# Squares two granules later, loads of weight pairs five granules behind their stores, and the threshold search's last sixteen bits every third granule

## The chip, the cores and the metric

The kernel runs on one core of one Trainium2 chip. The metric is the device time of one execution in microseconds (us), given as the median of three runs. One further execution was recorded by the hardware profiler, and all rows below come from it.

## What is computed

2048 tokens of 1024 values are normalised (xn) and go through two feed-forward networks, whose results are added to the token.

```python
s = silu(xn @ w_gate.T)                      # 2752 values a token
s = where(|s| among the 1376 smallest, 0, s) # per token
a = (s * (xn @ w_up.T)) @ w_down.T

shared = (relu(xn @ up_w) ** 2) @ down_w     # 2048 values a token
routed = ((xn @ fc1_w) @ expert_w * (sum of the two largest of xn @ gate_w)) @ fc2_w
y = x + a + layernorm(shared + routed) * gamma + beta
```

## The kernel before

**Blocks and granules.** The tokens are taken in four blocks of 512 (four tiles of 128). In each block TensorE goes through the same list `STEPS` of 212 granules. A granule is one slab of 128 rows by 512 columns of a weight and takes twelve matmuls (three for each tile: every 32-bit operand is held as a high part and a low part, and the products high by high, high by low and low by high are added). The steps that matter here, with their first granules: gate 0 to 5 from 0, latent 48, hidden 0 and 1 from 56, routed 72, shared 0 and 1 from 80, hidden 2 and 3 from 96, up 4 at 112, shared 2 and 3 from 120, up 0 at 136, up 1 at 144, up 2 at 152, up 3 at 160, out 0 at 168, out 1 at 190. Successive steps use PSUM banks 0 to 3 and 4 to 7 in turn, so up 2 can begin on its banks only when VectorE has read those of up 0.

**The weight pairs.** In block 0 a granule's weight arrives raw (a ring of `RAW` = 4) and is split into its two parts in a slot of the ring `w` (`RING` = 6 slots). ScalarE makes the high part (line 474), but for granules 52 to 167 GpSimd makes it (line 443); GpSimd always makes the low part (line 447) and signals `lo_ready`. SyncE's queue issues every transfer (lines 383 to 414): for each granule of block 0 it waits for `lo_ready`, loads the raw slab four granules ahead and stores the pair in DRAM (line 347, into `split_w`). Blocks 1 to 3 load the pairs from there (line 353) into the slot of the granule six before, once TensorE has read it; for the first six granules of block 1 that load also waits for the slot's own store.

**The other engines** run a loop over the same granule numbers m, each in its own order, and wait on semaphores; a number m on them is a place in their order, not a time. Results of a step that ends at granule e are read at m = e + 4 (`LAG`). `granule_read` is the wait for TensorE's reading.

- Squares of hidden values (`HIDDEN_AT`, m = 68, 70, ... 82 and 108, 110, ... 122, sixteen a block): ScalarE squares into the high part at m (line 531), GpSimd squares the same at full precision at m (line 452) and VectorE subtracts at m + 1 for the low part (line 935). TensorE's shared granules wait for that low part one by one (`hidden_lo`).
- The search (`SEARCH_AT`): 31 bits of a threshold for each token, one bit a step, starting at m = 52. In each step VectorE makes a candidate (line 808) and counts for tiles 0 and 1 (line 813, two passes), ScalarE counts for tiles 2 and 3 at m and m + 1 (line 486), and VectorE settles the bit (lines 798 and 801) at the next step's place. Bits 0 to 14 are three granules apart, the later ones three and four in turn, so that bit 30 is at 150 and `SEARCH_END` is 153.
- At `SEARCH_END` VectorE looks for ties (`drop_ties`, four counting passes at line 821 and a few small operations), then come the masks (`MASK_AT`, line 875), with up's results read in between (`READ_UP_AT`, line 788: up 4 at 123, up 0 at 147, up 1 at 155, up 2 at 163, up 3 at 169). Masks 4, 5, 0, 1 and 2 are at 154, 155, 156, 157 and 164.
- From m = 163 on GpSimd multiplies the masked values (line 463), TensorE turns them (line 606), ScalarE and VectorE take them back (lines 579 and 973), four granules ahead of out 0, which uses them.

Of the kernel before, what the change touches and what calls it, by code (L numbers as in the profile page):

```python
# [33 lines left out]
TILES = N // P  # L34
BLOCKS = TOKENS // N
# [9 lines left out]
RING = 6  # L45
RAW = 4
LAG = 4
BITS = 31
# [100 lines left out]
SEARCH_AT = {END[("gate", GC - 1)] + LAG + 1: 0}  # L149
while len(SEARCH_AT) < BITS:  # L150
    _last = max(SEARCH_AT)
    SEARCH_AT[_last + 3 + (len(SEARCH_AT) % 2 if len(SEARCH_AT) >= BITS // 2 else 0)] = len(SEARCH_AT)
SEARCH_FROM, SEARCH_END = min(SEARCH_AT), max(SEARCH_AT) + 3
MASK_AT = {max(SEARCH_END + 1 + i, END[("up", g)] + LAG + 1 if g < GC - 1 else 0): g
           for i, g in enumerate(GROUPS[:-1])}
# [4 lines left out]
assert len(GATED_AT) == GK and len(MASK_AT) == GC  # L160
READ_HIDDEN_AT = {END[("hidden", i)] + LAG: ("hidden", i) for i in range(SC)}
HIDDEN_AT = {END[("hidden", i)] + LAG + 1 + 2 * t: (i, t) for i in range(SC) for t in range(TILES)}
GPSIMD_HI = list(range(SEARCH_FROM, OUT0))
NORM_AT = [OUT0 + 6 + 3 * t for t in range(TILES)]
TOKENS_AT = [OUT0 + 20, OUT0 + 21, OUT1 + 10, OUT1 + 14]
# [9 lines left out]
def granule_read(eng, granule_used, bank_filled, b, m):  # L175

    if m in ENDS:
        name = next(s for s in END if END[s] == m)
        eng.wait_ge(bank_filled, filled(b, (*name, TILES - 1)))
    else:  # L180
        eng.wait_ge(granule_used, released(b, m))
# [19 lines left out]
def program(nc, x, w_gate, w_up, w_down, up_w, down_w, fc1_w, expert_w, fc2_w, gamma, beta, routed_w, y):  # L201
    ctx = ExitStack()
    with ctx:
# [133 lines left out]
        @block.sync  # L337
        def _(sp):
            def load_raw(m):
                src, width = source(m)  # L340
                if m == START[("routed", 0)]:
                    sp.wait_ge(routed_stored, 32)
                sp.dma_start(raw[:, m % RAW, 0:width], src).then_inc(raw_loaded[m % RAW], 16)

            def store_split(m):
                width = source(m)[1]
                sp.dma_start(split_w[m, :, :, 0:width],
                             w[:, m % RING, :, 0:width].bitcast(F32)).then_inc(split_stored[m % RING], 16)

            def load_split(g):  # L350
                m, r = g % GRANULES, g % RING
                width = source(m)[1]
                sp.dma_start(w[:, r, :, 0:width].bitcast(F32), split_w[m, :, :, 0:width]).then_inc(split_loaded[r], 16)

            def load_rows(b, t):
                sp.dma_start(rows_of(t), x[(b * TILES + t) * P:(b * TILES + t + 1) * P, :])\
                  .then_inc(rows_loaded[t % 2], 16)

            def store(b, i, t):

                s = slice(i * N, (i + 1) * N)
                bank, value = emptied(b, ("out", i, t))
                sp.wait_ge(bank_emptied[bank], value)
                sp.dma_start(y[(b * TILES + t) * P:(b * TILES + t + 1) * P, s], acc[:, t, s]).then_inc(stored, 16)

            for t in range(2):
                load_rows(0, t)
            for k in range(LK):
                sp.dma_start(expert_raw[:, k, :], expert_w[k * P:(k + 1) * P, :]).then_inc(first_loaded[k], 16)
                sp.dma_start(fc2_raw[:, k, :], fc2_w[k * P:(k + 1) * P, :]).then_inc(first_loaded[k], 16)  # L370
            for t in range(2, TILES):
                sp.wait_ge(bank_filled, FIRST_AT[("token", t - 2)] + 2)
                load_rows(0, t)
            for m in range(RAW):
                load_raw(m)
            sp.dma_start(gamma_all[:, :], gamma.to_broadcast([P, HID])).then_inc(consts_loaded, 16)
            sp.dma_start(beta_all[:, :], beta.to_broadcast([P, HID])).then_inc(consts_loaded, 16)
            for h in range(2):
                s = slice(h * N, (h + 1) * N)
                for t in range(LK):  # L380
                    sp.wait_ge(bank_emptied[4 + t], 2 + h)
                sp.dma_start(routed_w[:, s].rearrange("(k p) n -> p k n", p=P), acc[:, :, s]).then_inc(routed_stored, 16)
            for b in range(BLOCKS):
                for m in range(GRANULES):
                    if b == 0:
                        sp.wait_ge(lo_ready, m + 1)
                        if m + RAW < GRANULES:
                            load_raw(m + RAW)
                        store_split(m)
                    if b * GRANULES + m + RING in range(GRANULES, BLOCKS * GRANULES):  # L390
                        granule_read(sp, granule_used, bank_filled, b, m)
                        if b == 0:
                            sp.wait_ge(split_stored[m % RING], 16 * (m // RING + 1))
                        load_split(b * GRANULES + m + RING)
                    for t in range(TILES):

                        if m == RESIDUAL_LOAD[t]:
                            if t < 2:

                                sp.wait_ge(bank_filled, filled(b, ("routed", 1, TILES - 1)))  # L400
                            else:
                                sp.wait_ge(apply_step, b * 4 * TILES + 4 * (t - 1))
                            load_rows(b, t)
                        if m == OUT1 + LAG + 2 + t:
                            store(b, 0, t)

                        if m == TOKENS_LOAD[t] and b + 1 < BLOCKS:
                            if t < 2:
                                sp.wait_ge(apply_step, b * 4 * TILES + 4 * (t + 3))
                            else:  # L410
                                sp.wait_ge(bank_filled, filled(b, ("token", t - 2, 1)))
                            load_rows(b + 1, t)
                for t in range(TILES):
                    store(b, 1, t)
            sp.wait_ge(stored, 16 * (2 * TILES * BLOCKS + 1))


# [1 line left out]
        def _(pool):  # L419
# [15 lines left out]
            for b in range(BLOCKS):  # L435
                for m in range(GRANULES):
                    width = source(m)[1]
                    r = m % RING
                    words, hi, lo = raw[:, m % RAW, 0:width], w[:, r, 0, 0:width], w[:, r, 1, 0:width]
                    if b == 0:  # L440
                        if m in GPSIMD_HI:
                            split_slot_free(pool, m)
                            pool.tensor_scalar(hi, words, 1.0, 1.0, ALU.mult, ALU.mult).then_inc(gpsimd_hi, 1)  # L443
                            pool.wait_ge(gpsimd_hi, GPSIMD_HI.index(m) + 1)
                        else:
                            pool.wait_ge(hi_ready, scalar_his(m))
                        pool.tensor_tensor(lo, words, hi, ALU.subtract).then_inc(lo_ready, 1)  # L447
                    if m in HIDDEN_AT:
                        i, t = HIDDEN_AT[m]
                        pool.wait_ge(operand_hi, highs(b, "hidden", i * TILES + t + 1))  # L450
                        n = i % 2 * TILES + t
                        pool.tensor_tensor(squares[:, n, :], squares[:, n, :], squares[:, n, :],  # L452
                                           ALU.mult).then_inc(squared, 1)
                    if m in GATED_AT:
                        c = CHUNKS[GATED_AT[m]]
                        pool.wait_ge(masked, (b * GC + GROUPS.index(c // 4) + 1) * TILES)
                        if c == GK - 1:

                            pool.tensor_tensor(prod[:, c, :, LAST:P], prod[:, c, :, 0:LAST], mag[:, c, :, 0:LAST],
                                               ALU.mult).then_inc(doubled, 1)  # L460
                            pool.wait_ge(doubled, b + 1)
                        units = slice(0, P if c < GK - 1 else LAST)
                        pool.tensor_tensor(prod[:, c, :, units], prod[:, c, :, units], mag[:, c, :, units],  # L463
                                           ALU.mult).then_inc(prod_ready, 1)
# [229 lines left out]
        def _(dve):  # L694
# [231 lines left out]
            for b in range(BLOCKS):  # L926
                for m in range(GRANULES):
                    if m in READ_AT:
                        read_step(b, READ_AT[m])
                    if m - 1 in HIDDEN_AT:  # L930

                        i, t = HIDDEN_AT[m - 1]
                        n = i % 2 * TILES + t
                        dve.wait_ge(squared, b * SC * TILES + i * TILES + t + 1)
                        dve.tensor_tensor(hidden[1][:, n, :], squares[:, n, :], hidden[0][:, n, :],
                                          ALU.subtract).then_inc(hidden_lo, 1)
# [68 lines left out]
```

## Time and profile before

| what | value |
|---|---|
| runs | 2412.04 us median of 3 (2411.74 to 2412.51) |
| the profiled execution | 2412.13 us, span 2410.3 us, mean granted TensorE clock 0.996 |
| TensorE busy | 2373.4 us (98% of the span) |
| VectorE busy | 1519.5 us (63%) |
| ScalarE busy | 968.2 us (40%) |
| GpSimd busy | 584.3 us (24%), nearly all of its line 447 in block 0 |
| DMA | 529.04 MB, mean 219 GB/s |

The span runs from the first to the last instruction; what lies around it, 1.8 us, is in the execution's time but not in the span. A share of the span says how busy an engine is on average over four blocks, of which the first does the splitting besides. An engine's idle time costs only where another waits for it.

### The profile page before, as it was taken

Reading aid. Unit: us, or ns where it says so; the run is one execution under the profiler, and the core shown is the slowest. Engines: PE = TensorE matmul, PEld = TensorE weight load, DVE = VectorE, ACT = ScalarE, POOL = GpSimd, SP = SyncE. Lnnn points to the kernel's source line nnn. Section 1 sums busy time; section 2 is a strip of 40 time slices with the busy share of each in tenths; the row PEclk is TensorE's granted clock in tenths of the full one; section 3 lists DMA queues with packets and bytes.
Section 4 is the critical chain, followed back from the end, with each engine's and each line's share of the span. In section 5 each row is a group of like instructions: output and inputs, shape, how many; then the busy total and the mean of one; then the engine's idle time right before and its main releaser. Section 6 shows DMA issues by size and latency. Waiting matters only on the chain.

```text
span 2410.3 us, 27343 instructions
## 1 busy us (share of the span) xinstructions
PE 2373.4 (98%) x10720; PEld 1971.8 (82%) x10720; DVE 1519.5 (63%) x1757; ACT 968.2 (40%) x1049; POOL 584.3 (24%) x502
## 2 busy tenths in 40 slices
PE   8999999989999999999999999999999999999999
PEld 7888777877878888888888888888888888888887
DVE  3139999886201998888321399889731169988850
ACT  3347665322211787531110287651200148665010
POOL 5566868687200000004000010103100001010500
PEclk9999999999999999999999999999999999999999
DMA  7886868957765656665666666666566566566555
GB/s 274 327 290 232 311 230 320 305 184 288 252 235 187 198 192 193 193 211 178 220 230 195 191 195 195 193 210 193 194 227 208 188 197 193 194 195 213 184 187 179
DMA packets 168578, 529.04 MB, mean 219 GB/s; under 512 B 18176, under 2 KB 27392, under 8 KB 168448
## 3 DMA queue, kind: packets, MB, share of 16 engines
q1 hardware_dynamic: 168448, 527.28, 65.5%
q8 instruction: 85, 1.39, 0.2%
q14 instruction: 45, 0.37, 0.0%
HBM read 406.55 MB, written 120.65 MB: 219 GB/s over the span
## 4 chain that ended last, share of the span: by engine, by line
PE 88%; DVE 7%; POOL 2%; issue 2%; DVEq 1%; DMA 1%; ACT 0%; SPq 0%; POOLq 0%
PE bank L586 29%; PE bank L588 29%; PE bank L587 28%; DVE junk_v L813 2%; PE bank L606 1%; DVE prod L875 1%; POOL w L447 1%; DVEq L700 1%; DVE junk_v L821 1%; PE bank L597 1%; POOL w L443 0%; DVE prod L788 0%; DVE cand L808 0%; POOL squares L452 0%; DVE acc L893 0%
## 5 line engine op out<-in xcount | busy, mean ns | idle before, releaser
L813 DVE TENSOR_SCALAR_CACHE_REDUCE junk_v<-mag,cand 128x2816 bf16<-128x2816 f32 x248 | 780.3, 3146 | 9.0 <-DVE cand L808 0.2
L486 ACT ACTIVATE junk_s<-mag,cand 128x2816 uint8<-128x2816 f32 x248 | 655.6, 2643 | 323.8 <-DVE cand L808 314.7
L586 PE MATMUL bank<-w,tok 128*128 128x512 f32 (+1 forms) x1408 | 545.4, 387 | 8.3 <-DMA w<-split_w 3.6
L588 PE MATMUL bank<-w,tok 128*128 128x512 f32 (+1 forms) x1408 | 543.6, 386 | 0.0
L587 PE MATMUL bank<-w,tok 128*128 128x512 f32 (+1 forms) x1408 | 543.1, 386 | 0.0
L452 POOL TENSOR_TENSOR squares<-squares 128x512 f32<-128x512 f32 x64 | 67.5, 1057 | 1192.8 <-ACT hidden L531 1192.8
L447 POOL TENSOR_TENSOR w<-raw,w 128x512 fp32r<-128x512 f32 (+1 forms) x212 | 291.6, 1381 | 121.7 <-ACT w L474 112.1
L586 PEld LDWEIGHTS bank<-w,tok 128*128 128x128 f32 x1408 | 265.5, 189 | 60.9 <-DMA w<-split_w 5.3
L739 DVE TENSOR_SCALAR positive<-mag 128x2048 uint8<-128x2048 f32 (+2 forms) x28 | 27.6, 984 | 454.0 <-ACT mag L507 397.8
L588 PEld LDWEIGHTS bank<-w,tok 128*128 128x128 f32 x1408 | 265.1, 188 | 50.5
L587 PEld LDWEIGHTS bank<-w,tok 128*128 128x128 f32 x1408 | 265.5, 189 | 49.9
L586 PE MATMUL bank<-w,prod_t 128*128 128x512 f32 x672 | 269.3, 401 | 3.1 <-DVE prod_t L973 3.1
L588 PE MATMUL bank<-w,prod_t 128*128 128x512 f32 x672 | 262.9, 391 | 0.0
L587 PE MATMUL bank<-w,prod_t 128*128 128x512 f32 x672 | 261.9, 390 | 0.0
L587 PE MATMUL bank<-tok,w 128*128 128x512 f32 x640 | 249.0, 389 | 0.0
L586 PE MATMUL bank<-tok,w 128*128 128x512 f32 x640 | 249.0, 389 | 0.0
L588 PE MATMUL bank<-tok,w 128*128 128x512 f32 x640 | 249.0, 389 | 0.0
L463 POOL TENSOR_TENSOR prod<-prod,mag 128x512 f32<-128x512 f32 x88 | 129.9, 1498 | 344.3 <-DVE prod L875 344.0
L586 PE MATMUL bank<-w,hidden 128*128 128x512 f32 x512 | 200.1, 391 | 3.9 <-POOL w L447 3.9
L587 PE MATMUL bank<-w,hidden 128*128 128x512 f32 x512 | 199.9, 390 | 0.0
L588 PE MATMUL bank<-w,hidden 128*128 128x512 f32 x512 | 199.7, 390 | 0.0
L507 ACT ACTIVATE mag<-bank 128x512 f32<-128x512 f32 x80 | 47.5, 598 | 335.1 <-PE bank L588 330.4
(91 smaller groups left out, 2638.5 us busy)
## 6 DMA issues: line engine op xcount, KB each, us to landing
w<-split_w SPq DMA_DIRECT2D x612, 512.0 KB, 4.1
split_w<-w SPq DMA_DIRECT2D x204, 512.0 KB, 5.3
rows<-x_dram SPq DMA_DIRECT2D x32, 512.0 KB, 4.8
raw<-w_down_dram SPq DMA_DIRECT2D x44, 256.0 KB, 4.7
raw<-w_gate_dram SPq DMA_DIRECT2D x40, 256.0 KB, 4.9
raw<-w_up_dram SPq DMA_DIRECT2D x40, 256.0 KB, 3.2
w<-split_w SPq DMA_DIRECT2D x24, 392.0 KB, 3.4
raw<-up_w_dram SPq DMA_DIRECT2D x32, 256.0 KB, 4.4
```

Source lines behind the costliest of these rows:

```text
L447: pool.tensor_tensor(lo, words, hi, ALU.subtract).then_inc(lo_ready, 1)
L452: pool.tensor_tensor(squares[:, n, :], squares[:, n, :], squares[:, n, :], ALU.mult).then_inc(squared, 1)
L463: pool.tensor_tensor(prod[:, c, :, units], prod[:, c, :, units], mag[:, c, :, units], ALU.mult).then_inc(prod_ready, 1)
L486: act.activation(junk_s[:, :, :], mag[:, :, t, :], ACT.Sign, scale=-1.0, bias=cand[:, t:t + 1], accum_out=cnt[:, t:t + 1]).then_inc(counte ...
L507: act.activation(mag[:, 4 * i:4 * i + 4, t, :], banks[bank][:, :].rearrange("p (k n) -> p k n", n=P), ACT.Silu).then_inc(bank_emptied[bank ...
L586: pe.matmul(out, left[0], right[0], start=first, stop=False)
L587: pe.matmul(out, left[0], right[1], start=False, stop=False)
L588: return pe.matmul(out, left[1], right[0], start=False, stop=last)
L597: last = pe.transpose(banks[2 * (t % 2) + h][:, k * P:(k + 1) * P], rows_of(t)[:, (h * HK // 2 + k) * P:(h * HK // 2 + k + 1) * P], ident[ ...
L606: last = pe.transpose(banks[bank][:, t * P:(t + 1) * P], prod[:, c, t, :], ident[:, :])
L739: dve.tensor_scalar(positive[:, ks, :, ns], mag[:, ks, :, ns], 0.0, 2.0, ALU.is_ge, ALU.mult).then_inc(signs_done, 1)
L813: dve.tensor_scalar(junk_v[:, :, :], mag[:, :, t, :], cand[:, t:t + 1], float(1 - (GATED - KEPT)), ALU.is_lt, ALU.add, accum_out=cnt[:, t: ...
```

## The change

Three places are edited. The rule for `SEARCH_AT` puts each of the bits 15 to 30 three granules after the one before: bit 15 at 97, bit 18 at 106, bit 21 at 115, bit 24 at 124, bit 27 at 133, bit 30 at 142, `SEARCH_END` at 145; masks 4, 5, 0, 1 and 2 are then at 146, 147, 148, 156 and 164. Everything else that is placed by granule, READ_UP_AT among it, stays where it was. Second, GpSimd squares at m + 2 and VectorE subtracts at m + 3 of ScalarE's place m. Third, SyncE's loop over the granules g still stores at g in block 0, but deals with the load into the slot of granule g - 5 at g, and the four stores of out 1 move with it.

```diff
-    SEARCH_AT[_last + 3 + (len(SEARCH_AT) % 2 if len(SEARCH_AT) >= BITS // 2 else 0)] = len(SEARCH_AT)
+    SEARCH_AT[_last + 3] = len(SEARCH_AT)
...
+SQUARE_LAG = 2
+BEHIND = RING - 1
...
-            for b in range(BLOCKS):
-                for m in range(GRANULES):
+            for g in range(BLOCKS * GRANULES + BEHIND):
+
+                if g < GRANULES:
+                    sp.wait_ge(lo_ready, g + 1)
+                    if g + RAW < GRANULES:
+                        load_raw(g + RAW)
+                    store_split(g)
+                if g >= BEHIND and g - BEHIND + RING in range(GRANULES, BLOCKS * GRANULES):
+                    b, m = divmod(g - BEHIND, GRANULES)
+                    granule_read(sp, granule_used, bank_filled, b, m)
                     if b == 0:
-                        sp.wait_ge(lo_ready, m + 1)
-                        if m + RAW < GRANULES:
-                            load_raw(m + RAW)
-                        store_split(m)
-                    if b * GRANULES + m + RING in range(GRANULES, BLOCKS * GRANULES):
-                        granule_read(sp, granule_used, bank_filled, b, m)
-                        if b == 0:
-                            sp.wait_ge(split_stored[m % RING], 16 * (m // RING + 1))
-                        load_split(b * GRANULES + m + RING)
+                        sp.wait_ge(split_stored[m % RING], 16 * (m // RING + 1))
+                    load_split(g - BEHIND + RING)
+                if g - BEHIND in range(GRANULES - 1, BLOCKS * GRANULES, GRANULES):
                     for t in range(TILES):
-
+                        store((g - BEHIND) // GRANULES, 1, t)
+                if g not in range(GRANULES, GRANULES + BEHIND):
+                    b, m = divmod(g if g < GRANULES else g - BEHIND, GRANULES)
+                    for t in range(TILES):
                         if m == RESIDUAL_LOAD[t]:
...
-                for t in range(TILES):
-                    store(b, 1, t)
             sp.wait_ge(stored, 16 * (2 * TILES * BLOCKS + 1))
...
-                    if m in HIDDEN_AT:
-                        i, t = HIDDEN_AT[m]
+                    if m - SQUARE_LAG in HIDDEN_AT:
+                        i, t = HIDDEN_AT[m - SQUARE_LAG]
                         pool.wait_ge(operand_hi, highs(b, "hidden", i * TILES + t + 1))
...
-                    if m - 1 in HIDDEN_AT:
-
-                        i, t = HIDDEN_AT[m - 1]
+                    if m - SQUARE_LAG - 1 in HIDDEN_AT:
+
+                        i, t = HIDDEN_AT[m - SQUARE_LAG - 1]
```

## Rows read from the trace of the kernel before

**Rows 1.** Whom TensorE waited for over the whole span: total us, times, longest us.

```profile
PE bank L586 <- POOL w L447: 9.7, 6, 2.6
...
PE bank L606 <- DVE prod L788: 7.1, 1, 7.1
PE bank L586 <- DMA w<-split_w: 3.6, 2, 2.2
PE bank L586 <- DVE prod_t L973: 3.1, 3, 1.0
```

**Rows 2.** TensorE's timeline, first matmuls of granules: start us, us, instruction.

```profile
460.91 0.39 PE L586 MATMUL bank<-w,tok 128*128 128x512 f32 x1
...
517.04 0.39 PE L586 MATMUL bank<-w,prod_t 128*128 128x512 f32 x1
...
651.25 0.39 PE L586 MATMUL bank<-w,tok 128*128 128x512 f32 x1
...
679.19 0.39 PE L586 MATMUL bank<-w,tok 128*128 128x512 f32 x1
...
1066.16 0.39 PE L586 MATMUL bank<-w,tok 128*128 128x512 f32 x1
...
1241.82 0.39 PE L586 MATMUL bank<-w,tok 128*128 128x512 f32 x1
...
1263.58 0.39 PE L586 MATMUL bank<-w,tok 128*128 128x512 f32 x1
...
1650.55 0.39 PE L586 MATMUL bank<-w,tok 128*128 128x512 f32 x1
...
1696.00 0.39 PE L586 MATMUL bank<-w,prod_t 128*128 128x512 f32 x1
```

**Rows 3.** TensorE's timeline after block 0's longest wait.

```profile
502.40 1.12 PE L606 MATMUL bank<-ident,prod 128*128 128x128 f32 x4 [7.06 <-DVE prod L788]
...
505.02 0.63 PE L587 MATMUL bank<-w,tok 128*128 128x512 f32 x1
```

**Rows 4.** SyncE's queue at the end of block 0.

```profile
648.94 0.43 SPq L347 DMA_DIRECT2D split_w<-w  x1
654.07 0.32 SPq L353 DMA_DIRECT2D w<-split_w  x1
```

**Rows 5.** VectorE's timeline after block 0's search.

```profile
480.69 2.74 DVE L875 SCALAR_TENSOR_TENSOR prod<-mag,thr,prod 128x512 f32<-128x512 f32 x4 [4.56 <-issue]
483.35 2.47 DVE L788 SCALAR_TENSOR_TENSOR prod<-positive,bank 128x512 f32<-128x512 uint8 x4
```

**Rows 6.** Whom VectorE waited for between 285 and 480 us.

```profile
DVE hidden L935 <- POOL squares L452: 4.0, 2, 2.9
```

**Rows 7.** VectorE's line 808 in a stretch of block 0 and of block 2: window, us, busy us.

```profile
306.00:462.00 156.00, 14.76 (x16) 0.99 0.81 284
1490.00:1644.00 154.00, 2.73 (x16) 1.00 0.63 199
```

**Rows 8.** GpSimd in a stretch of block 0: window, us, busy us.

```profile
298.00:481.00 183.00, 133.11 (x137) 0.99 0.82 286
```

**Rows 9.** ScalarE's reading of a hidden step's banks, in block 1.

```profile
933.76 2.64 ACT L519 ACTIVATE squares<-bank 128x512 f32<-128x512 f32 x4 [3.98 <-PE bank L588]
```

**Rows 10.** VectorE's timeline in block 1: candidates 14, 15 and 30, and the first mask.

```profile
900.46 0.17 DVE L808 TENSOR_SCALAR cand<-thr 128x4 int32<-128x4 int32 x1
...
907.58 0.17 DVE L808 TENSOR_SCALAR cand<-thr 128x4 int32<-128x4 int32 x1
...
1052.78 0.17 DVE L808 TENSOR_SCALAR cand<-thr 128x4 int32<-128x4 int32 x1
...
1077.29 2.74 DVE L875 SCALAR_TENSOR_TENSOR prod<-mag,thr,prod 128x512 f32<-128x512 f32 x4 [3.76 <-issue]
```

**Rows 11.** VectorE's subtractions for the hidden low parts (line 935), block 2.

```profile
1490.00:1644.00 154.00, 7.06 (x8) 1.00 0.63 199
```

## The prediction

> **What bounds the kernel now.** I read first whom TensorE waited for, since it is busy 98% of the span. Leaving out the start-up, four kinds of wait are left [rows 1]: on GpSimd's low parts (9.7 us in six waits), on VectorE's reading of up's banks (7.1), on the loads of weight pairs (3.6) and on VectorE's turned products (3.1). Then I took TensorE's timeline and looked up the first matmul of each granule, by counting twelve matmuls a granule [rows 2]. Block 2 shows no wait, so it is the measure: its gate 0 takes 1263.58 - 1241.82 = 21.76 us, 2.72 us a granule. The same eight granules of block 1 take 679.19 - 651.25 = 27.94 us. So the whole of what can be won lies in block 0 and at the head of block 1; blocks 1 to 3 are otherwise at TensorE's pace, and there the change can only lose. The timeline after the long wait shows a matmul of 0.63 us where 0.39 is usual [rows 3]: that is the clock at 1.2 instead of 2.4 GHz. The first granule after it took 1.4 us more than block 2's. Last I read VectorE in block 0. It goes from one operation to the next all through the search; between 285 and 480 us it waits for an engine only twice, 4.0 us in all, for squares [rows 6]. In block 0 the search is thus paced by VectorE's own work and not by its places in the order. That decides this change.
>
> **Loads apart from stores.** At the end of block 0 each store is issued right behind the load before it, which itself waits for TensorE to read a granule, and the next load waits for that store to land: store at 648.94, load at 654.07 [rows 4], so a load every 5.4 us where TensorE needs one every 2.72. With the loads five granules behind, all six stores go out on `lo_ready`, some five granules ahead of the reading that the load waits for (13.6 us against 5.1 from store to load). The loads then follow TensorE's reading. The four stores of out 1 stay behind the load for the slot of granule 211 and wait for VectorE's additions as now; the load queued behind them is needed 13.6 us later, which covers it. Block 1's head returns to 21.76: **-6.2 us**. If contention in the DMA queues kept some of it, 0 to -6.2 are the bounds; I take the full value, as nothing else waits there.
>
> **Squares two granules later.** GpSimd now splits two more granules before it waits for ScalarE's square. This gives TensorE 5.4 us more of supply against waits on GpSimd of 2.6 us at most [rows 1], so most of the 9.7 us goes, with the slow matmuls behind it. It is worth nothing by itself, because TensorE only arrives earlier at the place below. The low parts come later by two granules on VectorE; in block 0 they then sit behind one more search step, and I expect waits of TensorE at granules 86, 125 and 127 in their place. These too are absorbed below. In blocks 1 to 3 they have 6 us to spare by the sum further down.
>
> **The search closed up.** This moves `SEARCH_END`, the tie check and mask 4 ahead of the reading of up 0 (147). Up 2, from granule 152, needs the banks of up 0. So in block 0 TensorE's granule 152 now waits for the end of the whole search, the ties, mask 4 and the first read of up 0, just as granule 160 now waits for up 1. The sum for VectorE in block 0: mask 4 starts at 480.69 [rows 5]. One reading of four banks leaves the chain, -2.5 [rows 5]. The waits for squares go, as GpSimd is done before VectorE comes, -4.0 [rows 6]. Bit 18 now has ScalarE's reading of hidden 2 (2.64 us of four, [rows 9]) between its two counts: ScalarE then takes about 1.2 us longer than VectorE's two passes, +1.2. The other subtractions are only dealt out differently over the steps; that I put at 0, between -2 and +2. One gain is left: the candidate on line 808 takes 14.76 us for sixteen in block 0 and 2.73 in block 2 [rows 7], 12 us more, and what differs is GpSimd, busy 133 of 183 us there [rows 8] and nearly idle in the other. TensorE now waits eight granules earlier, so eight splits of 2.0 us fall behind the chain: 16/133 of 12 us is 1.5, and with the two settling operations, which are lengthened too, I take **-2.0**. Mask 4 starts at 480.7 - 2.5 - 4.0 + 1.2 - 2.0 = 473.4. Its four operations take 2.7 and the first read of up 0 0.7 [rows 5]: granule 152 begins at 476.8. Before it began at 460.91 [rows 2], and freed from the waits on GpSimd it could come by 451 at the latest. So TensorE waits some 26 us or more in all before granule 152, wherever that falls.
>
> From there to out 0 block 2 takes 1696.00 - 1650.55 = 45.45 us [rows 2], and the clock's fall costs 1.4 once. Up 1 is read well before granule 160, so the old waits at 160 and 164 do not return. Out 0 begins at 476.8 + 1.4 + 45.45 = 523.7, before 517.04 [rows 2]: **+6.6 us**. Behind that, VectorE's norms and turned products stand to TensorE as before, so the 3.1 us of waits stay (0; bounds -4 and +2).
>
> By the Trainium skill, TensorE: Matmul & The Clock Gate, Part 1, the array falls to half its clock after idling and must be busy a while to get it back. The trace agrees, with the 0.63 us matmul [rows 3]. By that rule each new short wait costs more than its length, but what it costs before granule 152 is swallowed by the long wait there.
>
> **Blocks 1 to 3.** Candidate 14 of block 1 is at 900.46 and a bare step takes 7.12 us [rows 10]. Sixteen steps are 113.9. Four readings (shared 1, up 4, shared 2, shared 3) are 9.9, by the 2.47 of [rows 5]. Eight subtractions are 7.1 [rows 11], and I add 1.7 for GpSimd's squares beside them. Bit 18 waits for TensorE's hidden 2, as ScalarE's reading waits for it [rows 9]: 1.4. From candidate 30 to the first mask are 24.5 [rows 10], and the mask and the first read 3.4. The sum is 900.5 + 113.9 + 9.9 + 8.8 + 1.4 + 24.5 + 3.4 = 1062.4, and granule 152 starts at 1066.16 [rows 2]. There are 3.8 us of cover, so I cost these blocks at 0. If the cover were gone, each block would pay the shortfall and 1.4 for the clock.
>
> **The sum.** 2412.1 (this execution; the median is 2412.04) - 6.2 + 6.6 = **2412.5 us**: no change. What was won for three kinds of wait is paid again at granule 152. About 0.2% (4.8 us) is what a measurement of this kernel can tell from no change.
>
> **Rivals.**
> A: VectorE's chain is shortened by much more, since GpSimd stands idle whenever TensorE waits. For it: the lengthened candidates cost 12 us [rows 7]. Against it: GpSimd must still make every low part before 157. If some 9 us more are shed, out 0 begins at 514.7, and the time is 2412.5 - 9 = 2403.5. The Trainium skill, SBUF — State Buffer, says the port pair of VectorE and GpSimd is an exclusive lock, the loser of which blocks until the other's instruction ends. The trace agrees as far as it goes, with the candidate at 0.92 us on average beside 0.17 [rows 7], and by that rule an idle GpSimd frees VectorE entirely.
> B: slower. In blocks 1 to 3 the 3.8 us of cover do not hold, and granule 152 waits for up 0 there too. It decides once VectorE's chain is over 3.8 us longer than my sum. At 7 us longer each block pays 3.2 + 1.4 = 4.6, three times 13.8: 2426. For it: the reading of up 0 has moved behind 24.5 us of ties. Against it: the chain has only known terms.
> C: the search in block 0 does keep its places, so that the waits on GpSimd and on up's banks (9.7, 7.1) go with their slow matmuls, about 25 us, and with the loads 31: 2381. Against it: VectorE's lack of any idle time [rows 6].
> D: the loads stay late, as the pairs' traffic collides with the last stores: 2412.5 + 6.2 = 2418.7.
>
> **How the numbers follow.** Forecast 0.57, with its own range 2408 to 2417 from the bounds of the dealing-out, the contention and out 0. A 0.2, B 0.13, C 0.05, D 0.05. The range takes in A and D and leaves out B and C, 0.18: 2403 to 2419. Faster by over 0.2% means under 2407.2: most of A, C and a little of the forecast, 0.28. Slower means over 2416.9: B, D and the forecast's edge, 0.21. Within is 0.51.
>
> **What the changed profile would show.** No wait of TensorE on a pair's load at block 1's head, and a 21.8 us gate 0 there. In block 0 a wait on line 788 before granule 152, with mask 4 near 473 and out 0 near 524. The 9.7 us of waits on line 447 mostly changed for waits on it at other granules and on line 935. No waits in blocks 1 to 3. The forecast is wrong if mask 4 of block 0 starts before 468 or after 478, or if any later block waits.

## The result and the profile after

| what | before | after |
|---|---|---|
| median of the runs | 2411.75 us (20 runs, 2410.55 to 2414.63) | 2415.57 us (20 runs, 2414.3 to 2419.55) |
| ratio | | 1.0016, 95% interval 1.0009 to 1.0023 |
| span of the profiled execution | 2410.3 us | 2413.8 us |

The changed kernel is 3.8 us slower. The interval leaves out 1, but the difference is under the 0.2% that was called measurable. The measured time lies in the forecast's range, 2403 to 2419, and 3.1 us above its middle, 2412.5. In the changed file lines up to 150 are unmoved, SyncE's load is on line 355, and what lay behind the queue's loop is five lines further on (VectorE's reading of up, 788, is now 793; the mask, 875, is 880).

TensorE's waits over the whole span, as [rows 1]:

```profile
PE bank L591 <- POOL w L452: 12.1, 5, 5.6
...
PE bank L591 <- DVE hidden L940: 7.3, 2, 5.8
PE bank L591 <- DVE prod L793: 6.9, 1, 6.9
PE bank L591 <- DVE prod_t L978: 3.1, 3, 1.0
```

The wait for a pair's load is gone, and so are the two for up at granules 160 and 164. In their place stand a wait for up of 6.9 us at another granule, where the longest was 7.1, then 7.3 us for the hidden low parts, which there were none of, and 2.4 us more for splits.

The first matmuls of granule 152 and of out 0 in block 0, and of the first and the ninth granule of block 1, as [rows 2]:

```profile
478.63 0.76 PE L591 MATMUL bank<-w,tok 128*128 128x512 f32 x1 [6.89 <-DVE prod L793]
...
526.69 0.39 PE L591 MATMUL bank<-w,prod_t 128*128 128x512 f32 x1
...
660.92 0.39 PE L591 MATMUL bank<-w,tok 128*128 128x512 f32 x1
...
682.68 0.39 PE L591 MATMUL bank<-w,tok 128*128 128x512 f32 x1
```

Granule 152 begins 17.7 us later than before, out 0 9.65 us later, and the head of block 1 takes 21.76 us in place of 27.94. That is the whole result: 9.65 - 6.18 = 3.5 us, the difference of the spans. Of the 9.65 us, 0.64 had gone by at the first granule of all, which began at 38.02 us and not at 37.38.

VectorE's timeline in block 0 between the counts of bit 18 and its settling, and behind the ties, as [rows 5]:

```profile
340.26 0.16 DVE L803 SCALAR_TENSOR_TENSOR step<-cnt,cand 128x4 f32<-128x4 f32 x1 [0.99 <-ACT junk_s L491]
...
475.15 2.74 DVE L880 SCALAR_TENSOR_TENSOR prod<-mag,thr,prod 128x512 f32<-128x512 f32 x4 [4.68 <-issue]
477.81 2.47 DVE L793 SCALAR_TENSOR_TENSOR prod<-positive,bank 128x512 f32<-128x512 uint8 x4
```

VectorE begins mask 4 at 475.15, 5.5 us earlier than before, and TensorE's granule 152 starts 0.8 us after the first of the four reads of up 0 began. It gets through its own work sooner, yet TensorE is later, since the work has moved ahead of a read that TensorE needs eight granules earlier.

SyncE's queue at the end of block 0, as [rows 4]. The last stores go out one after another with no load between them, and the loads then follow TensorE's reading:

```profile
638.12 8.18 SPq L349 DMA_DIRECT2D split_w<-w  x5
646.62 14.81 SPq L355 DMA_DIRECT2D w<-split_w  x6
```

The same in block 1: candidate 14 (line 813), mask 4 and the read of up 0, as [rows 10]:

```profile
903.95 0.17 DVE L813 TENSOR_SCALAR cand<-thr 128x4 int32<-128x4 int32 x1
...
1059.04 2.74 DVE L880 SCALAR_TENSOR_TENSOR prod<-mag,thr,prod 128x512 f32<-128x512 f32 x4 [3.78 <-issue]
1061.69 2.47 DVE L793 SCALAR_TENSOR_TENSOR prod<-positive,bank 128x512 f32<-128x512 uint8 x4
```

Granule 152 of block 1 starts at 1069.65, 7.3 us after the first of these reads (0.7 us long) is done, so the later blocks lose nothing.

### The profile page after: what moved, and what is told of

It reads as the page before. It is cut to its first block, busy times and chain, and to the rows that moved or that the text cites. A ratio compares the mean times of both kernels' runs of the same rounds, so it can differ in the third digit from the quotient of the medians.

```text
span 2413.8 us, 27343 instructions
## 1 busy us (share of the span) xinstructions
PE 2372.6 (98%) x10720; PEld 1972.4 (82%) x10720; DVE 1503.1 (62%) x1757; ACT 967.2 (40%) x1049; POOL 579.8 (24%) x502
## 4 chain that ended last, share of the span: by engine, by line
PE 84%; DVE 13%; issue 1%; DVEq 1%; ACT 0%; DMA 0%; POOL 0%
PE bank L591 27%; PE bank L593 27%; PE bank L592 27%; DVE junk_v L818 7%; PE bank L611 1%; DVE cand L813 1%; DVE step L803 1%; DVEq L705 1%; DVE junk_v L826 1%; PE bank L602 1%; DVE thr L806 0%; DVE acc L898 0%; DVE prod L880 0%; DVE acc L788 0%; DVE acc L904 0%
## 5 line engine op out<-in xcount | busy, mean ns | idle before, releaser
L584 ACT ACTIVATE prod_t<-bank 128x512 fp32r<-128x512 f32 x88 | 52.2, 595 | 384.7 <-PE bank L611 384.7
L468 POOL TENSOR_TENSOR prod<-prod,mag 128x512 f32<-128x512 f32 x88 | 122.3, 1411 | 337.7 <-DVE prod L880 337.4
```

The lines of the kernel that those rows point to most:

```text
L584: act.activation(prod_t[0][:, c, :], banks[bank][:, :], ACT.Copy).then_inc(operand_hi, 1)
```

## The experiments: each part alone, and both winners together

The theory: the search's closing up is the loser and the other two parts are winners. The rival: the squares' lag is the loss, as TensorE's 7.3 us of waits for hidden low parts suggest. Each of the kernels was timed against the kernel before.

**Loads alone**, the kernel before with SyncE's new loop.

```diff
-    SEARCH_AT[_last + 3] = len(SEARCH_AT)
+    SEARCH_AT[_last + 3 + (len(SEARCH_AT) % 2 if len(SEARCH_AT) >= BITS // 2 else 0)] = len(SEARCH_AT)
...
-SQUARE_LAG = 2
+SQUARE_LAG = 0
```

This diff is against the changed kernel.

> Kernel before with the loads five granules behind the stores, nothing else. Theory (the search's closing up is the loser, the loads and the squares are winners): gate 0 of block 1 takes 21.8 us in place of 27.9, all else as before; 6.2 us less than before, ratio 0.9974. Rival (the loads' own traffic costs elsewhere): 0 to 3 us less, with a new wait in block 0.

Measured: 2405.94 us beside 2412.13, ratio 0.9975 (0.9966 to 0.9984): 6.2 us less, as expected. Its waits in block 0 are nearly those of the kernel before (9.6 us for splits in five waits, 1.4 and 7.1 for up).

**Squares alone**, against the kernel before.

```diff
-                    if m in HIDDEN_AT:
-                        i, t = HIDDEN_AT[m]
+                    if m - 2 in HIDDEN_AT:
+                        i, t = HIDDEN_AT[m - 2]
                         pool.wait_ge(operand_hi, highs(b, "hidden", i * TILES + t + 1))
...
-                    if m - 1 in HIDDEN_AT:
-
-                        i, t = HIDDEN_AT[m - 1]
+                    if m - 3 in HIDDEN_AT:
+
+                        i, t = HIDDEN_AT[m - 3]
```

> Kernel before with the squares two granules later, nothing else. Theory (VectorE's chain sets block 0): the waits for splits shrink from 9.7 us to under 6, but TensorE gains only what VectorE no longer waits for squares, 4 us, since granules 160 and 164 wait for VectorE; ratio 0.9983. Rival (the waits for low parts, 7.3 us in the changed kernel, come from the squares' lag and are the loss): slower than before by 3 to 7 us.

Measured: 2409.65 us, ratio 0.9987 (0.9978 to 0.9996): 2.5 us less. TensorE's waits:

```profile
PE bank L586 <- DMA w<-split_w: 6.2, 3, 2.5
PE bank L586 <- DVE prod L788: 6.0, 1, 6.0
PE bank L606 <- DVE prod L788: 5.4, 1, 5.4
...
PE bank L586 <- DVE hidden L935: 2.6, 2, 1.5
PE bank L586 <- POOL w L447: 0.7, 1, 0.7
```

The rival falls. The waits for splits shrink from 9.7 to 0.7 us and 2.6 us for low parts appear, but TensorE's gain until granule 152 (9.5 us, by the starts of that granule) is mostly given back at up: 6.0 us at granule 160, where 1.3 us stood, for VectorE is the one that is late. Block 0 ends 3.9 us earlier. That this is so near the 4.0 us of [rows 6] is partly luck: VectorE waits for no square any more, but mask 4 starts 4.8 us earlier, as VectorE's small operations changed in length too (the part on why the prediction was right has them for the changed kernel). The rest of the expected gain was lost at the head of block 1, where the loads still stand behind the stores and which took 2.5 us more than before in this execution. Why 2.5 us more was not looked into.

**Search alone**, the kernel before with the one line of the search.

```diff
-    SEARCH_AT[_last + 3 + (len(SEARCH_AT) % 2 if len(SEARCH_AT) >= BITS // 2 else 0)] = len(SEARCH_AT)
+    SEARCH_AT[_last + 3] = len(SEARCH_AT)
```

> Kernel before with the last sixteen bits three granules apart, nothing else. Theory: granule 152 of block 0 waits for the first read of up 0 behind ties and mask 4, near 479 us, as in the changed kernel; the loads' 6.2 us are missing, so 9 to 12 us slower than before, ratio 1.004 to 1.005. Rival: within 3 us of before.

Measured: 2424.84 us, ratio 1.0049 (1.0036 to 1.0062): 12.7 us slower, a little over the expected 9 to 12. Mask 4 starts at 479.12 and the wait on line 788 is at granule 152:

```profile
PE bank L586 <- DVE prod L788: 9.6, 1, 9.6
```

**Loads and squares**, the changed kernel with the search's old line (the diff above, turned round).

> Changed kernel with the search's old places, everything else kept. Theory: 6.2 + 4 = 10 us less than before (ratio 0.9957), 14 less than the changed kernel, and no wait at granule 152. Rival (the squares' lag is the loss): near the changed kernel, 2412 us or more.

Measured: 2402.01 us, ratio 0.9956 (0.9943 to 0.9969): 10.1 us less than before, to the figure expected. The three parts alone come to -6.2 - 2.5 + 12.7 = +4.0 us, and the whole change to +3.8. That this sum comes out is partly luck, for the pairs don't add up: loads and squares are 1.4 us better together than their sum of -8.7, and loads and search, below, come to +4.4 where the sum is +6.5. Beside the other two parts the closed-up search costs 2415.57 - 2402.01 = 13.6 us.

## The experiments: where the search's loss sits

**Up 0 read first**: VectorE reads up 0's banks at 144, ahead of the ties and mask 4.

```diff
-READ_UP_AT = {END[("up", g)] + (2 if g == GROUPS[-1] else LAG): ("up", g) for g in range(GC - 1)}
+READ_UP_AT = {END[("up", g)] + (2 if g == GROUPS[-1] else 1 if g == 0 else LAG): ("up", g) for g in range(GC - 1)}
```

> Changed kernel with VectorE reading up 0 at 144, ahead of the ties and mask 4, in place of 147. Theory: granule 152 of block 0 no longer waits (7.05 us and 2.5 for the clock), nothing takes its place, as up 1 is read near 486 us and granule 160 comes at 493; 9.6 us less than the changed kernel: 2406. The waits for low parts and splits ahead of granule 152 stay. Rival (those earlier waits are the loss, the one at 152 only their echo): within 3 us of the changed kernel.

Measured: 2405.57 us, ratio 0.9973 (0.9962 to 0.9983), 10.0 us less than the changed kernel where 9.6 were expected. It is one number in the order of VectorE's work. Mask 4 now starts later than in the changed kernel, and that harms nothing:

```profile
477.52 13.58 DVE L880 SCALAR_TENSOR_TENSOR prod<-mag,thr,prod 128x512 f32<-128x512 f32 x12 [5.08 <-issue]
```

The waits ahead of granule 152 are still there (12.2 us for splits, 5.7 for low parts), so what was recovered is the loss at 152: 10.0 of the 13.6 us. The other 3.6 us show at out 0, which begins at 516.81 here and at 513.24 with loads and squares, though here TensorE waits for nothing between granule 127 and out 0. So they come from the waits ahead of 152, most of which the closed-up search makes as well. The longest for a split, 5.6 us at granule 111, begins on GpSimd:

```profile
340.82 1.04 POOL L457 TENSOR_TENSOR squares<-squares 128x512 f32<-128x512 f32 x1 [16.73 <-ACT hidden L536]
```

This is the changed kernel. GpSimd splits nothing for 16.73 us, until ScalarE has squared the first of hidden 2, which it does at 340.11, after it has counted for bit 18. With loads and squares alone, that square begins at 332.89, ahead of the counting for bit 18, GpSimd's wait is 9.83 us and TensorE has no wait at 111.

**No search for ties.** This kernel leaves out `drop_ties` in every block, so tokens with equal values at the threshold are not settled as the reference does.

```diff
-SEARCHES = searched(BITS) + TILES + 4
+SEARCHES = searched(BITS)
...
-                        drop_ties(b)
```

> Changed kernel that leaves out the search for ties (four counting passes and what follows) in every block. Theory: mask 4 of block 0 starts some 18.6 us earlier, but only the wait at granule 152 goes, 9.6 us: 2406, as with up 0 read first. Rival (VectorE's chain sets block 0's end whole): 18 us less, 2397.

Measured: 2406.42 us, ratio 0.9975 (0.9965 to 0.9986). Mask 4 of block 0 starts at 457.13, 18 us earlier, and the kernel gains 9.2 us, nearly as much as by reading up 0 first. The rival's 2397 is missed. Taking 18 us out of the late engine is worth what TensorE waits behind it and nothing more.

**Loads and search**, the changed kernel with `SQUARE_LAG = 0`.

> Changed kernel with the squares back at their old places. Theory: the parts add up, so the closed-up search (+12.7) and the loads (-6.2) give 2418.5, 3 us slower than the changed kernel. Rival (the lag of squares costs once the search is closed up): faster than the changed kernel.

Measured: 2416.72 us, ratio 1.0017 (1.0008 to 1.0026). Set against the time before in its own comparison it is 4.4 us slower where the changed kernel was 3.8. So the squares' lag, worth 2.5 to 4 us with the old search, is worth 0.6 to 1.2 us beside the closed-up one: what is saved at the splits (17.5 us of waits here against 12.1) TensorE waits for at the low parts (none here against 7.3), and the wait at granule 152 is 6.9 us in both. Neither the expected 3 us nor a loss was seen.

## The experiments: a version that beats both

With loads and squares alone, two waits at up are left (6.0 us at granule 160 and 5.4 at the turned product behind 163, in both executions). They are waits behind ties and masks.

**Reads first**, on loads and squares: up 1 read ahead of the ties, up 2 ahead of masks 0 and 1.

```diff
-READ_UP_AT = {END[("up", g)] + (2 if g == GROUPS[-1] else LAG): ("up", g) for g in range(GC - 1)}
+READ_UP_AT = {END[("up", g)] + (2 if g in (1, 2, GROUPS[-1]) else LAG): ("up", g) for g in range(GC - 1)}
...
-MASK_AT = {max(SEARCH_END + 1 + i, END[("up", g)] + LAG + 1 if g < GC - 1 else 0): g
-           for i, g in enumerate(GROUPS[:-1])}
+MASK_AT = {SEARCH_END + 1: GROUPS[0], SEARCH_END + 2: GROUPS[1], 162: 0, 163: 1, 164: 2}
```

> Loads and squares as changed, the search at its old places; VectorE reads up 1 at 153, ahead of the ties, and up 2 at 161, ahead of masks 0 and 1, which go to 162 and 163. Theory: of the waits at granules 160 (6.2 and 1.7 for the clock) and 164 (6.0 and 2.3) only some 3 us at 164 are left: 8 to 13 us less than loads and squares alone, 2389 to 2394. Rival (masks 0 and 1, now later, or GpSimd's products become the wait): 2398 or more.

Measured: 2405.41 us, ratio 0.9966 (0.9952 to 0.998). The theory failed here and the rival was right: it is no faster than loads and squares alone (its five runs lie between 2402.44 and 2405.75).

```profile
PE bank L590 <- DVE prod_t L977: 13.4, 7, 5.5
```

The waits at up are all but gone (0.9 us), and in their place TensorE waits for turned products. They stand behind three masks that VectorE now does in one run, seen in its timeline:

```profile
486.71 17.46 DVE L879 SCALAR_TENSOR_TENSOR prod<-mag,thr,prod 128x512 f32<-128x512 f32 x12
504.10 1.87 DVE L977 TENSOR_TENSOR prod_t<-bank,prod_t 128x512 fp32r<-128x512 f32 x3
```

The same order made the later blocks wait too, which they never had: by the starts of their granules, blocks 1, 2 and 3 take 3.8, 2.3 and 3.8 us more than with loads and squares alone. Block 0 is 6.4 us shorter, so it is these blocks that turn a gain into a loss.

**Masks spread**, against reads first.

```diff
-MASK_AT = {SEARCH_END + 1: GROUPS[0], SEARCH_END + 2: GROUPS[1], 162: 0, 163: 1, 164: 2}
-MASK_AT[OUT0 + 3] = GROUPS[-1]
+MASK_AT = {SEARCH_END + 1: 4, SEARCH_END + 2: 5, 162: 0, 168: 1, 171: 2, 173: 3}
```

> As e8_reads_first, with the masks dealt out among the turned products: mask 0 at 162, 1 at 168, 2 at 171, 3 at 173, so that VectorE takes back turned products 0 and 1 behind mask 0 alone. Theory: the waits on turned products before out 0 (5.7 us and 2.5 for the clock in block 0, 3.8 in block 1, 2.2 in block 2) go and 0 to 4 us of waits for the later masks come back: 2390 to 2396. Rival (VectorE simply has too much to do between granules 160 and 184 of block 0, in whatever order): 2400 or more, with the waits further on.

Measured: 2397.55 us, ratio 0.9939 (0.9925 to 0.9953): 14.2 us less than before and 4.5 less than loads and squares alone, the fastest version of this study (its five runs, 2396.87 to 2398.02, lie apart from those of loads and squares, 2401.56 to 2402.7, though the two ratios' intervals overlap a little). It misses the expected range by 1.5 us. Blocks 1 to 3 lose nothing again, and in block 0 the long wait is cut into short ones, ten in all with the three that stood there before:

```profile
PE bank L589 <- DVE prod_t L976: 10.3, 10, 1.8
```

**The same with a lag of one granule** (`SQUARE_LAG = 1`).

> As e9_spread with the squares one granule later in place of two. Theory: the waits for low parts (2.6 us and 1.7 for the clock) shrink and waits for splits come back in part (9.7 us without a lag, 0.7 with two); as VectorE's chain covers them up to granule 163, within 3 us of e9_spread. Rival: one is clearly better, by over 3 us.

Measured: 2398.19 us, ratio 0.9939 (0.9925 to 0.9954). The lag of one or two makes no difference that can be measured.

## Why the prediction was right, point by point

- **Loads apart from stores, -6.2.** 6.18 us in the changed kernel's trace and 6.2 alone. No part was kept by the queues.
- **Squares two granules later, absorbed.** Right in kind. The new waits are at granules 83, 86, 111, 119, 123, 125 and 127, of which 86, 125 and 127 were named (125 waits for a split, not for a low part). Only those at 83 and 86 belong to the lag alone: with the old search the next is one of 1.1 us at 126. The others, from 111 on, need the closed-up search, which the forecast had not reckoned with, since it had put all of the search's price at granule 152.
- **The search closed up.** The mechanism was right: the first read of up 0 sets granule 152. Of the sum's terms, ScalarE's reading between two counts was put at 1.2 and cost a wait of 0.99 us. The waits for squares, 4.0, are all gone. Mask 4 came at 475.15 where 473.4 was said, 1.75 us later. Behind candidate 14 the sum was good, and a little too long: from there to mask 4 VectorE took 175.24 us in place of 183.30, 8.1 less where the terms came to 7.3. The relief from GpSimd, put at 2.0 (16/133 of 12 is 1.4 and not 1.5), measured 2.5 there, over the candidates and both settling operations. The miss came ahead of candidate 14, where the forecast had put nothing. 0.64 us is the later first granule. The other 1.9 are in the first settling operation (line 798, now 803), its busy time here from the first candidate to candidate 14, before and after:

```profile
168.70:297.35 128.65, 8.28 (x14) 0.99 0.78 274
169.35:299.88 130.53, 10.21 (x14) 1.00 0.82 285
```

  It is the squares' lag that does this: the stretch from candidate 0 to 14 takes 130.5 us with a lag of two granules, in all seven traces, and 128.5 to 128.8 with a lag of one or none. Why that operation is longer then was not tested.
- **The clock's fall, 1.4.** Too small. Granule 152 was 2.5 us longer than block 2's, with all of its twelve matmuls slow, where seven were in the case of [rows 3]. Even there the clock had cost 1.8 us and not 1.4, for the four transposes ahead of the seven were slow too (from 502.40 to out 0 it took 14.64 us, and 12.81 in block 2).
- **From granule 152 to out 0.** Nothing took the place of the old waits, as said. Out 0 began at 526.69 where 523.7 was said, the 3.0 us being the two points above (1.8 and 1.1). They make up nearly all of the 3.1 us between the forecast and the time. In the 1.8 us two errors partly cancel (1.9 too little ahead of candidate 14, 0.8 too much behind it), which was luck.
- **Turned products, 0.** 3.1 us in three waits, as before.
- **Blocks 1 to 3, 0.** Right. The cover is 7.3 us and not 3.8: from candidate 14 to mask 4 they take 155.1 us where the sum had 158.5.
- **The rivals.** A (a chain shorter by 9 us) is shown wrong by mask 4's time, B by the cover, C by the waits that stayed, D by the head of block 1. So the mechanism was right and not only the number, but the closed-up search has a second cost, the waits ahead of granule 152, that the forecast let the long wait swallow. It did swallow it here; it came to light, as 3.6 us, when up 0 was read first.

## What to carry to other kernels

When an engine is late, its place numbers no longer give times: what counts is the order of its work, and what stands ahead of the operation that another engine waits for. Before moving long work forward on such an engine, list each read that it passes and when the waiting engine needs that read; moving one short read (2.5 us) ahead of 22 us of work (455.9 to 477.8 us in the changed kernel) returned 10 us here. Test the parts of a compound change alone, for two of three were worth 10 us and the third cost 13.

## What was not expected of the hardware

- The time at half the clock after a wait varied, after waits of much the same length: 1.8 us were lost after a wait of 7.1 us [rows 3], 2.5 after 6.9 us in the changed kernel and 3.0 after 5.9 us (granule 109 with loads and search). After waits of 2.6 us in block 0 it was anything from 0.1 us (granules 117 and 123 with the search alone) to 3.0 (granule 81 there). The granted clock, third from the end of this line, is 0.51 of the full one over granule 152 of the changed kernel:

```profile
478.60:484.00 5.40, 5.37 (x13) 4.24 (x14) 5.40 (x11) 0.00 (x0) 0.00 (x0) 0.51 0.02 3
```

- The execution's start-up moved by up to 1.4 us between kernels that are alike there (granule 0 at 37.37 us with loads and search, 38.79 with the search alone), so single profiles can't settle differences of one microsecond in this kernel unless they are counted from the first granule.
